# Folding the four squared-deviation subsets on GpSimd before the averaging matmul

## Chip, cores and metric

One core of a Trainium2 chip runs the whole program. The metric is the device time of one launch in microseconds.

## What is computed

The input `x` is 32 images of 512 channels, 28 x 28 pixels, float32. The reference, cut to what matters:

```python
def _gn(v, G=32, eps=1e-05):                       # group norm: 16 channels and all pixels of one image
    m = jnp.mean(g, axis=(2, 3, 4), keepdims=True)
    s = jnp.var(g, axis=(2, 3, 4), keepdims=True)
    return (g - m) / jnp.sqrt(s + eps)
...
xa = round(clip((xg - lA) / (uA - lA), 0, 1) * 15) / 15      # xg: the normed input, channel groups rotated by one
wq = (round(clip((weight - lW) / (uW - lW), 0, 1) * 15) / 15 - 0.5) * 2
y = einsum('bgihw,goi->bgohw', xa, wg)                       # 4 groups of 128 x 128, 1 x 1 convolution
y = relu(y * inv + shift)                                     # batch norm with given statistics
return x + (y + identity)                                     # identity: the normed input
```

## The kernel before, in words

Channels lie on the 128 partitions, in 4 groups (G) of 784 pixels per image. The images go through a ring of 12 buffers, `images`. Loads and the last two images' stores are issued by SyncE (L192, L200, L204, L213), the stores of images 0 to 29 by ScalarE (L263). A load beyond the twelfth waits until the store of the image that had its buffer has landed (L199).

The norm is worked out for two images at a time, a pair `u`. Per pair:

- VectorE takes partial statistics of 2 of the 4 groups (3 for the first two pairs) with `bn_stats` (L461) on half images. Each half gives two subsets, so a group has SUBSETS = 4 partial means and partial sums of squares. `sum_stats` (L469) adds them. ScalarE takes the sum and the squares of the other groups (L237, L243).
- TensorE averages across the 16 channels of a norm group with small float32 matmuls: `average_means` (L576, L577, L579). ScalarE copies the means to SBUF (L251, `gmean`).
- GpSimd takes the deviations of the subset means from the group mean (`deviations`, L376 and L379) and squares them (L383). TensorE averages the squares into `var_ps`, one matmul for each of the four subsets (`average_deviations`, L585). ScalarE forms the standard deviation (L257, L258), VectorE a rough reciprocal (L493), GpSimd refines it and forms the coefficients in seven small instructions (`coefficients`, L399 to L407).
- Per image and group, ScalarE (L271, three groups) and GpSimd (L425, one group) write int16 levels. VectorE caps them to bf16 codes, four groups at once (`cap`, L476). TensorE multiplies (`multiply`, L612, six matmuls: three parts of the weight by two halves). GpSimd turns the image into the normed one plus the input (`affine`, L414); in the last four images ScalarE does two of four (L279). VectorE adds the convolution (`finish`, L483).

`average_deviations(u)` stands in TensorE's queue between the first and the second group of an image. `keep_busy` (L593) adds six matmuls per pair whose result nobody reads. Each engine runs its own list in order, written out by hand:

- GpSimd, iteration n: coefficients (every second image), the first affine, then every second image `deviations`, the other affines, `quantise` of the next image.
- VectorE, image n: finish 0, finish 1, cap of the next image, finish 2, one half of statistics, finish 3, three halves.

A small GpSimd instruction that reads the result of the one before it waits on a semaphore for it (`linked`, L387).

Of the kernel before, what the change touches and what calls it, by code (L numbers as in the profile page):

```python
# [5 lines left out]
ALU = mybir.AluOpType  # L6
ACT = mybir.ActivationFunctionType
AXIS = mybir.AxisListType
F32 = mybir.dt.float32
# [3 lines left out]
P = 128  # L13
# [13 lines left out]
SUBSETS = 4  # L27
# [4 lines left out]
def fused_norm_quantised_conv(nc, x, weight, limits, channel_params, out):  # L32

    B, C, H, W = x.shape
    G = CONV_GROUPS
# [11 lines left out]
    def stats_on_dve(u):  # L47
        return 3 if u < 2 else 2
# [21 lines left out]
    def squares_until(u):  # L70
        return sum(2 * (G - stats_on_dve(i)) for i in range(u + 1))
# [10 lines left out]
    with ExitStack() as ctx:  # L82
        def sb(name, shape, dtype):
            return ctx.enter_context(nc.sbuf_tensor(name, shape, dtype))

        def ps(name, shape, dtype):
            return ctx.enter_context(nc.psum_tensor(name, shape, dtype))

        def sem(name):
            return ctx.enter_context(nc.semaphore(name))  # L90
# [8 lines left out]
        unused = sb("unused", [P, 2, HW], BF16)  # L99
        gmean = sb("gmean", [P, 2, 2, G], F32)  # L100
        dev = sb("dev", [P, 2, G, SUBSETS], F32)
        dev2 = sb("dev2", [P, 2, G, SUBSETS], F32)
        half_var = sb("half_var", [P, 2 * G], F32)
        std = sb("std", [P, 2, G], F32)
        rough = sb("rough", [P, 2, G], F32)
# [26 lines left out]
        avg = sb("avg", [P, P], F32)  # L132
# [5 lines left out]
        var_ps = ps("var_ps", [P, 512], F32)  # L138
# [26 lines left out]
        dev_step = sem("dev_step")  # L165
        dev_done = sem("dev_done")
        var_done = sem("var_done")
# [20 lines left out]
        @block.sync  # L188
        def _(sync):
            for n in range(SINGLE):  # L190
                for g in (0, G - 1, 1, 2):
                    sync.dma_start(images[:, n, g], x_v[n][:, g]).then_inc(first_loaded[n][g], DMA)  # L192
                if n == 0:
                    sync.dma_start(w_raw[:], weight.rearrange("(g o) i -> o g i", o=P)).then_inc(weights_in, DMA)

            def load(n):
                j = n % RING
                if n >= RING:
                    sync.wait_ge(stored[j], DMA * (n // RING))  # L199
                sync.dma_start(images[:, j], x_v[n]).then_inc(x_loaded[j], DMA)  # L200

            def store(n):
                sync.wait_ge(final, G * n + G)
                sync.dma_start(out_v[n], images[:, n % RING]).then_inc(stored[n % RING], DMA)  # L204

            for n in range(SINGLE, B):
                load(n)
            for n in range(ACT_STORES, B - 1):
                store(n)
            for g in range(G):  # L210
                o = output_group(g)
                sync.wait_ge(final, G * (B - 1) + g + 1)
                sync.dma_start(out_v[B - 1][:, o], images[:, (B - 1) % RING, o]).then_inc(stored[(B - 1) % RING], DMA)  # L213
            for j in range(RING):
                stores = len(range(j, B, RING)) + (G - 1 if j == (B - 1) % RING else 0)
                sync.wait_ge(stored[j], DMA * stores)
# [113 lines left out]
        def _(pool):  # L330
            step = [0]

            def chained(ins):
# [33 lines left out]
                                    cols[:, 1].unsqueeze(1).to_broadcast([P, 2, G]),  # L367
                                    bn[:, 4].unsqueeze(1).to_broadcast([P, 2, G]), ALU.subtract)

            def deviations(u):  # L370
                k, par = stats_on_dve(u), u % 2
                pool.wait_ge(gmean_done, u + 1)
                if u >= 1:
                    pool.wait_ge(var_done, u)
                mean = gmean[:, par].unsqueeze(3)
                nc.gpsimd.tensor_tensor(dev[:, :, 0:k], stats[:, par, :, 0:k, :, 1],  # L376
                                        mean[:, :, 0:k].to_broadcast([P, 2, k, SUBSETS]), ALU.subtract)
                own = sums[:, par, 0].unsqueeze(3)
                nc.gpsimd.tensor_tensor(dev[:, :, k:G], own[:, :, k:G].to_broadcast([P, 2, G - k, SUBSETS]),  # L379
                                        mean[:, :, k:G].to_broadcast([P, 2, G - k, SUBSETS]),  # L380
                                        ALU.subtract).then_inc(dev_step, 1)
                pool.wait_ge(dev_step, u + 1)
                nc.gpsimd.tensor_tensor(dev2[:], dev[:], dev[:], ALU.mult).then_inc(dev_done, 1)  # L383

            LINKS = 6

# [172 lines left out]
        @block.tensor  # L559
        def _(pe):  # L560
            pe.wait_ge(consts_done, 1)
            pe.wait_ge(rows_in, DMA)
            nc.tensor.transpose(cols_ps[:, 0:4 * G], rows[:], ident[0:4 * G, 0:4 * G])
            pe.wait_ge(limits_in, DMA)
            nc.tensor.matmul(cols_ps[:, 4 * G:5 * G], one_row[:], limit_row[:], start=True,
                             stop=True).then_inc(cols_turned, 1)

            def average_means(u):
                k, par = stats_on_dve(u), u % 2
                pe.wait_ge(bn_summed, u + 1)  # L570
                pe.wait_ge(squared, squares_until(u))
                if u >= 1:
                    pe.wait_ge(gmean_done, u)
                    pe.wait_ge(std_done, u)
                mean = mean_ps[:, 0:2 * G].rearrange("p (j g) -> p j g", g=G)
                nc.tensor.matmul(mean[:, :, 0:k], avg[:], sums[:, par, 0, :, 0:k], start=True, stop=True)  # L576
                nc.tensor.matmul(mean[:, :, k:G], avg_one[:], sums[:, par, 0, :, k:G], start=True,  # L577
                                 stop=True).then_inc(mean_done, 1)
                nc.tensor.matmul(var_ps[:, 0:2 * G], avg_n[:], sums[:, par, 1], start=True, stop=False)  # L579

            def average_deviations(u):
                pe.wait_ge(dev_done, u + 1)
                var = var_ps[:, 0:2 * G].rearrange("p (j g) -> p j g", g=G)
                for s in range(SUBSETS):
                    done = nc.tensor.matmul(var, avg[:], dev2[:, :, :, s], start=False, stop=(s == SUBSETS - 1))  # L585
                done.then_inc(var_done, 1)

            def keep_busy(n, u):  # L590
                pe.wait_ge(gmean_done, u)
                for _ in range(FILLERS):
                    nc.tensor.matmul(mean_ps[:, 0:HALF], w_t[:, 0, 0], codes[:, n % 2, G - 1, 0:HALF], start=True, stop=True)  # L593


            def wait_affine(n, g):
                if g < G - affine_on_act(n):
                    pe.wait_ge(y_pool, (y_pool_until(n - 1) if n else 0) + g + 1)
                else:
                    pe.wait_ge(y_act, y_act_until(n - 1) + g - (G - affine_on_act(n)) + 1)  # L600

            def multiply(n, g):
                k = G * n + g
                if g == 0:
                    pe.wait_ge(capped, n + 1)
                if k >= SETS:
                    pe.wait_ge(final, k - SETS + 1)
                for part in range(PARTS):
                    for h in range(2):
                        if (part, h) == (PARTS - 1, 1):  # L610
                            wait_affine(n, g)
                        done = nc.tensor.matmul(prod[:, k % SETS, h, 0:HALF], w_t[:, part, output_group(g)],  # L612
                                                codes[:, n % 2, g, h * HALF:(h + 1) * HALF],
                                                start=(part == 0), stop=(part == PARTS - 1))
                done.then_inc(multiplied, 1)

            pe.wait_ge(w_scaled, 1)
            for g in range(G):
                turned = nc.tensor.transpose(prep_ps[:, g], w_raw[:, g], ident[:])
            turned.then_inc(w_turned, 1)  # L620
            average_means(0)
            average_deviations(0)
            pe.wait_ge(w_ready, 1)

            for n in range(-1, B - 1):
                if n < 0:
                    average_means(1)
                    multiply(0, 0)
                    average_deviations(1)
                    multiply(0, 1)  # L630
                    multiply(0, 2)
                else:
                    multiply(n + 1, 0)
                    if n % 2 and (n + 3) // 2 < PAIRS:
                        average_deviations((n + 3) // 2)
                    multiply(n + 1, 1)
                    multiply(n + 1, 2)
                    if n % 2 == 0 and (n + 4) // 2 < PAIRS:
                        keep_busy(n + 1, (n + 4) // 2)
                        average_means((n + 4) // 2)  # L640
                multiply(n + 1, 3)
# [23 lines left out]
```

## Time and profile before

| | |
|---|---|
| median of 3 runs (lowest to highest) | 258.94 us (258.55 to 259.93) |
| the profiled execution: its own time | 260.06 us |
| the profiled execution: span from first to last instruction | 258.3 us |
| VectorE, GpSimd, ScalarE busy | 234.5, 213.8, 215.8 us (91%, 83%, 84%) |
| TensorE busy (matmuls) | 181.7 us (70%) |
| moved by DMA | 103.25 MB, mean 400 GB/s |

Busy shares are means over the whole span, the start and the end with little in them included. All times inside the trace count from the first instruction.

### The profile page before, as it was taken

Reading aid. Unit: us, or ns where it says so; the run is one execution under the profiler, and the core shown is the slowest. Engines: PE = TensorE matmul, PEld = TensorE weight load, DVE = VectorE, ACT = ScalarE, POOL = GpSimd, SP = SyncE. Lnnn points to the kernel's source line nnn. Section 1 sums busy time; section 2 is a strip of 40 time slices with the busy share of each in tenths; the row PEclk is TensorE's granted clock in tenths of the full one; section 3 lists DMA queues with packets and bytes.
Section 4 is the critical chain, followed back from the end, with each engine's and each line's share of the span. In section 5 each row is a group of like instructions: output and inputs, shape, how many; then the busy total and the mean of one; then the engine's idle time right before and its main releaser. Section 6 shows DMA issues by size and latency. Waiting matters only on the chain.

```text
span 258.3 us, 3631 instructions
## 1 busy us (share of the span) xinstructions
PE 181.7 (70%) x1083; PEld 106.4 (41%) x1083; DVE 234.5 (91%) x363; ACT 215.8 (84%) x394; POOL 213.8 (83%) x340
## 2 busy tenths in 40 slices
PE   1142978687778778686868787777868687799800
PEld 0132635354444445352535444443525353455400
DVE  2898698999999999999999999999999999999910
ACT  4338898999999999999999999999999889979300
POOL 6126869999999999999999999999999999989100
PEclk9999999999999999999999999999999999999975
DMA  6999999999999999999999999999999999999992
GB/s 224 393 412 410 408 408 408 415 418 417 416 415 417 417 413 417 416 416 416 415 418 417 414 416 417 417 414 416 416 418 413 416 417 411 401 397 403 400 399 97
DMA packets 34516, 103.25 MB, mean 400 GB/s; under 512 B 1202, under 2 KB 1730, under 8 KB 34498
## 3 DMA queue, kind: packets, MB, share of 16 engines
q1 hardware_dynamic: 18624, 54.86, 53.5%
q10 hardware_dynamic: 15874, 48.18, 46.7%
q8 instruction: 8, 0.13, 0.2%
q14 instruction: 10, 0.08, 0.1%
HBM read 51.65 MB, written 51.38 MB: 399 GB/s over the span
## 4 chain that ended last, share of the span: by engine, by line
DVE 77%; issue 7%; POOL 4%; PE 4%; DMA 2%; DVEq 0%; SPq 0%; ACT 0%; ACTq 0%; POOLq 0%
DVE images L483 41%; DVE stats L461 21%; DVE codes L476 12%; DMA images<-in_x 2%; PE prod L612 2%; PE var_ps L585 2%; DVE sums L469 1%; POOL images L414 1%; POOL levels L425 1%; DVE rough L493 1%; POOL newt L399 0%; DVEq L82 0%; DVE w_raw L519 0%; SPq L192 0%; POOL dev L379 0%
## 5 line engine op out<-in xcount | busy, mean ns | idle before, releaser
L612 PE MATMUL prod<-codes,w_t 128*128 128x392 bf16 x768 | 144.8, 334 | 43.4 <-DVE codes L476 22.6
L483 DVE SCALAR_TENSOR_TENSOR images<-prod,floor,images 128x784 f32<-128x784 f32 x128 | 126.6, 1014 | 2.8 <-PE prod L612 2.8
L414 POOL TENSOR_SCALAR images<-images,coef 128x784 f32<-128x784 f32 x120 | 119.3, 1009 | 0.0
L612 PEld LDWEIGHTS prod<-codes,w_t 128*128 128x128 bf16 x768 | 70.3, 102 | 110.9 <-DVE codes L476 34.4
L271 ACT ACTIVATE levels<-images,coef 128x784 int16<-128x784 f32 x95 | 91.5, 1028 | 0.9 <-issue 0.9
L461 DVE BATCH_NORM_STATS2 stats<-images 128x6 f32<-128x392 f32 x136 | 68.7, 548 | 5.3 <-DMA images<-in_x 5.3
L237 ACT ACTIVATE unused<-images 128x784 bf16<-128x784 f32 x60 | 50.8, 847 | 7.2 <-DMA images<-in_x 5.2
L243 ACT ACTIVATE unused<-images,sums 128x784 bf16<-128x784 f32 x60 | 56.1, 939 | 0.1
L476 DVE TENSOR_SCALAR codes<-levels 128x3136 bf16<-128x3136 int16 x32 | 40.8, 1275 | 1.2 <-POOL levels L425 1.2
L425 POOL TENSOR_SCALAR levels<-images,coef 128x784 int16<-128x784 f32 x33 | 33.1, 1005 | 0.1
L376 POOL TENSOR_TENSOR dev<-stats,gmean 128x16 f32<-128x16 f32 (+1 forms) x16 | 15.2, 948 | 9.2 <-ACT gmean L251 9.2
L585 PEld LDWEIGHTS var_ps<-dev,avg 128*128 128x128 f32 x128 | 18.1, 209 | 2.7 <-POOL dev L383 1.5
L585 PE MATMUL var_ps<-dev,avg 128*128 128x8 f32 x128 | 16.9, 259 | 1.4 <-POOL dev L383 1.4
L593 PE MATMUL mean_ps<-codes,w_t 128*128 128x392 bf16 x84 | 16.2, 329 | 0.0
L403 POOL TENSOR_TENSOR norm<-gmean,norm 128x8 f32<-128x8 f32 x16 | 14.5, 904 | 1.3
L243 ACT ACTIVATION_READ_ACCUMULATOR unused<-images,sums 128x1 f32 x60 | 11.4, 191 | 0.0
L237 ACT ACTIVATION_READ_ACCUMULATOR unused<-images 128x1 f32 x60 | 11.3, 188 | 0.0
L257 ACT ACTIVATE half_var<-var_ps,eps 128x8 f32<-128x8 f32 x16 | 4.3, 267 | 7.4 <-PE var_ps L585 7.4
L593 PEld LDWEIGHTS mean_ps<-codes,w_t 128*128 128x128 bf16 x84 | 8.2, 98 | 4.8
L576 PE MATMUL mean_ps<-sums,avg 128*128 128x4 f32 (+1 forms) x32 | 5.1, 230 | 6.8 <-DVE sums L469 6.8
L576 PEld LDWEIGHTS mean_ps<-sums,avg 128*128 128x128 f32 x32 | 6.0, 205 | 8.2 <-issue 4.9
L399 POOL TENSOR_TENSOR newt<-rough 128x8 f32<-128x8 f32 x16 | 4.0, 249 | 5.5 <-DVE rough L493 5.5
(68 smaller groups left out, 88.8 us busy)
## 6 DMA issues: line engine op xcount, KB each, us to landing
images<-in_x SPq DMA_DIRECT2D x30, 1568.0 KB, 13.3
out<-images ACTq DMA_DIRECT2D x30, 1568.0 KB, 18.9
images<-in_x SPq DMA_DIRECT2D x8, 392.0 KB, 6.6
out<-images SPq DMA_DIRECT2D x1, 1568.0 KB, 11.0
out<-images SPq DMA_DIRECT2D x4, 392.0 KB, 8.0
w_raw<-in_weight SPq DMA_DIRECT2D x1, 256.0 KB, 6.6
rows<-in_channel_params ACTq DMA_DIRECT2D x1, 8.0 KB, 2.4
limit_row<-in_limits ACTq DMA_DIRECT2D x1, 0.0 KB
```

Of the source, the lines that this page charges most:

```text
L237: nc.scalar.activation(unused[:, g % 2], images[:, n % RING, g], ACT.Identity, scale=1.0 / HW, accum_out=sums[:, u % 2, 0, j, g:g + 1]).th ...
L243: nc.scalar.activation(unused[:, g % 2], images[:, n % RING, g], ACT.Square, scale=-1.0, bias=sums[:, u % 2, 0, j, g:g + 1], accum_out=sum ...
L271: nc.scalar.activation(levels[:, n % 2, g], images[:, n % RING, g], ACT.Relu, bias=coef[:, u % 2, 1, 0, G * j + g:G * j + g + 1], scale=co ...
L376: nc.gpsimd.tensor_tensor(dev[:, :, 0:k], stats[:, par, :, 0:k, :, 1], mean[:, :, 0:k].to_broadcast([P, 2, k, SUBSETS]), ALU.subtract)
L414: nc.gpsimd.tensor_scalar(here, here, coef[:, u % 2, 0, 1, G * j + o:G * j + o + 1], coef[:, u % 2, 1, 1, G * j + o:G * j + o + 1], ALU.mu ...
L425: nc.gpsimd.tensor_scalar(levels[:, n % 2, g], images[:, n % RING, g], coef[:, u % 2, 0, 0, G * j + g:G * j + g + 1], coef[:, u % 2, 1, 0, ...
L461: nc.vector.bn_stats(two, images[:, n % RING, g, h * HALF:(h + 1) * HALF]).then_inc(bn_done, 1)
L476: nc.vector.tensor_scalar(codes[:, n % 2], levels[:, n % 2], 0.0, TOP, ALU.max, ALU.min).then_inc(capped, 1)
L483: nc.vector.scalar_tensor_tensor(out=two, in0=prod[:, k % SETS, :, 0:HALF], scalar=floor[:, o:o + 1], in1=two, op0=ALU.max, op1=ALU.add).t ...
L585: done = nc.tensor.matmul(var, avg[:], dev2[:, :, :, s], start=False, stop=(s == SUBSETS - 1))
L593: nc.tensor.matmul(mean_ps[:, 0:HALF], w_t[:, 0, 0], codes[:, n % 2, G - 1, 0:HALF], start=True, stop=True)
L612: done = nc.tensor.matmul(prod[:, k % SETS, h, 0:HALF], w_t[:, part, output_group(g)], codes[:, n % 2, g, h * HALF:(h + 1) * HALF], start= ...
```

## The change

GpSimd's `deviations` gets two more instructions: after the square, subsets 0 and 1 are added to subsets 2 and 3 (32 elements to 16 per partition), and the two halves are added (16 to 8). Each waits for the one before it. TensorE's `average_deviations` then is one float32 matmul and no longer four.

```diff
-        dev2 = sb("dev2", [P, 2, G, SUBSETS], F32)
+        dev2 = sb("dev2", [P, 2 * G, SUBSETS], F32)
+        dev2_half = sb("dev2_half", [P, 2 * G, SUBSETS // 2], F32)
+        dev2_sum = sb("dev2_sum", [P, 2 * G], F32)
...
+            FOLDS = 3
+
+            def folded(u, k, ins):
+                ins.then_inc(dev_step, 1)
+                pool.wait_ge(dev_step, FOLDS * u + k)
...
-                nc.gpsimd.tensor_tensor(dev[:, :, k:G], own[:, :, k:G].to_broadcast([P, 2, G - k, SUBSETS]),
-                                        mean[:, :, k:G].to_broadcast([P, 2, G - k, SUBSETS]),
-                                        ALU.subtract).then_inc(dev_step, 1)
-                pool.wait_ge(dev_step, u + 1)
-                nc.gpsimd.tensor_tensor(dev2[:], dev[:], dev[:], ALU.mult).then_inc(dev_done, 1)
+                folded(u, 1, nc.gpsimd.tensor_tensor(dev[:, :, k:G], own[:, :, k:G].to_broadcast([P, 2, G - k, SUBSETS]),
+                                                     mean[:, :, k:G].to_broadcast([P, 2, G - k, SUBSETS]), ALU.subtract))
+                dev_ = dev[:].rearrange("p j g s -> p (j g) s")
+                folded(u, 2, nc.gpsimd.tensor_tensor(dev2[:], dev_, dev_, ALU.mult))
+                folded(u, 3, nc.gpsimd.tensor_tensor(dev2_half[:], dev2[:, :, 0:2], dev2[:, :, 2:4], ALU.add))
+                nc.gpsimd.tensor_tensor(dev2_sum[:], dev2_half[:, :, 0], dev2_half[:, :, 1], ALU.add).then_inc(dev_done, 1)
...
-                var = var_ps[:, 0:2 * G].rearrange("p (j g) -> p j g", g=G)
-                for s in range(SUBSETS):
-                    done = nc.tensor.matmul(var, avg[:], dev2[:, :, :, s], start=False, stop=(s == SUBSETS - 1))
-                done.then_inc(var_done, 1)
+                nc.tensor.matmul(var_ps[:, 0:2 * G], avg[:], dev2_sum[:], start=False, stop=True).then_inc(var_done, 1)
```

`keep_busy` and everything else stay as they are.

## Rows read from the trace of the kernel before

**Rows 1.** The page: the chain that ended last, by engine.
```profile
DVE 77%; issue 7%; POOL 4%; PE 4%; DMA 2%; DVEq 0%; SPq 0%; ACT 0%; ACTq 0%; POOLq 0%
```

**Rows 2.** Busy time of each engine in one pair's stretch, 127.05 to 141.10 us.
```profile
core 0: us, PE busy (x) PEld busy (x) DVE busy (x) ACT busy (x) POOL busy (x), PEclk, DMA share, GB/s
127.05:141.10 14.05, 11.04 (x68) 6.36 (x68) 14.02 (x22) 13.38 (x26) 13.50 (x21) 1.00 1.03 417
```

**Rows 3.** The same view, long stretches: steady part, its end, after the last issue.
```profile
41.10:214.00 172.90, 135.94 (x841) 78.58 (x841) 172.23 (x257) 163.41 (x306) 166.24 (x247) 1.00 1.03 416
214.00:240.00 26.00, 21.97 (x133) 12.09 (x130) 25.34 (x35) 24.59 (x39) 24.56 (x36) 1.00 1.03 402
...
247.75:258.30 10.55, 0.00 (x0) 0.00 (x0) 0.00 (x0) 0.00 (x0) 0.00 (x0) 0.55 0.55 214
```

**Rows 4.** DMA rate in 40 slices of 0.38 us, from 243.2 to 258.3 us.
```profile
GB/s 399 390 399 399 407 399 407 399 399 399 399 399 399 399 399 407 391 424 407 399 407 391 357 341 316 324 249 100 75 58 25 25 25 25 25 25 17 0 0 0
```

**Rows 5.** Stores and loads: issues (start us), landings, the chain's first transfer.
```profile
out<-images ACTq DMA_DIRECT2D x30, 1568.0 KB, 18.9
...
L204 SPq DMA_DIRECT2D out<-images x1: 388/388/388, 242.6 to 242.6; - x1
...
L213 SPq DMA_DIRECT2D out<-images x4: 356/866/1252, 243.5 to 246.5; - x4
...
DMA to landing us min/median/max: 7.6/8.0/11.1
...
0.79 1.81 SPq L192 DMA_DIRECT2D images<-in_x  x4
...
1.70 5.65 DMA images<-in_x
```

**Rows 6.** Timeline of GpSimd and VectorE in one pair (start us, us, engine, line).
```profile
125.52 1.01 POOL L414 TENSOR_SCALAR images<-images,coef 128x784 f32<-128x784 f32 x1
125.80 1.60 DVE L476 TENSOR_SCALAR codes<-levels 128x3136 bf16<-128x3136 int16 x1
126.48 1.00 POOL L376 TENSOR_TENSOR dev<-stats,gmean 128x16 f32<-128x16 f32 x1
...
127.73 0.24 POOL L383 TENSOR_TENSOR dev<-dev 128x32 f32<-128x32 f32 x1
127.95 2.96 POOL L414 TENSOR_SCALAR images<-images,coef 128x784 f32<-128x784 f32 x3
...
132.98 1.07 POOL L403 TENSOR_TENSOR norm<-gmean,norm 128x8 f32<-128x8 f32 x1
133.03 0.96 DVE L476 TENSOR_SCALAR codes<-levels 128x3136 bf16<-128x3136 int16 x1
...
138.58 1.01 POOL L425 TENSOR_SCALAR levels<-images,coef 128x784 int16<-128x784 f32 x1
...
139.84 1.60 DVE L476 TENSOR_SCALAR codes<-levels 128x3136 bf16<-128x3136 int16 x1
```

**Rows 7.** Groups by line: a small linked GpSimd instruction (busy, mean ns, idle before).
```profile
L400 POOL TENSOR_TENSOR newt<-newt,half_var 128x8 f32<-128x8 f32 x16 | 3.3, 206 | 1.3
```

**Rows 8.** Timeline: TensorE at the start and in a pair, and who waits.
```profile
18.23 1.87 PE L585 MATMUL var_ps<-dev,avg 128*128 128x8 f32 x8 [1.45 <-POOL dev L383]
...
26.89 2.14 PE L612 MATMUL prod<-codes,w_t 128*128 128x392 bf16 x6 [0.54 <-DVE codes L476]
...
28.82 1.71 PE L585 MATMUL var_ps<-dev,avg 128*128 128x8 f32 x8
...
33.77 0.82 POOL L399 TENSOR_TENSOR newt<-rough 128x8 f32<-128x8 f32 x1 [2.47 <-DVE rough L493]
...
127.46 1.17 PE L612 MATMUL prod<-codes,w_t 128*128 128x392 bf16 x6 [0.87 <-DVE codes L476]
...
128.46 0.95 PE L585 MATMUL var_ps<-dev,avg 128*128 128x8 f32 x8
...
227.80 0.27 ACT L257 ACTIVATE half_var<-var_ps,eps 128x8 f32<-128x8 f32 x1 [1.31 <-PE var_ps L585]
```

## Prediction

> **What bounds the kernel now.** I read the chain that ended last first. It gives VectorE 77% and DMA 2% [rows 1]. Taken alone, that says a VectorE-bound kernel. The windows by engine say more. One pair of images takes 14.05 us, and VectorE is busy for 14.02 of it [rows 2]. I read six such stretches between 43 and 226 us; all are 14.04 or 14.05 us long. GpSimd is busy for 13.50 us. The rest, 0.55 us, is the seven gaps of about 0.08 us in its linked instructions (1.3 us over 16 pairs for each such line [rows 7]). So GpSimd never waits for anybody either. Two engines are full at once.
>
> The timeline shows why. The cap (L476) takes 0.96 us at 133.03 but 1.60 us at 125.80, where a GpSimd affine began at 125.52 and ended at 126.53. The cap was done 0.87 us after that end, at 127.40. The GpSimd instruction behind the affine, 16 elements per partition, took 1.00 us, from 126.48 to 127.48 [rows 6]. Each of the two has to wait until the other's instruction is over. VectorE loses some 0.7 us per pair in this, counted as busy, so its own work is about 13.3 us. GpSimd loses about 0.8 us twice per pair (L376 and L403), and it cannot avoid that. **GpSimd, not VectorE, sets the 14.05 us.**
>
> The third reading is DMA. It is full (share 1.03) from 41.1 to 214 us at 416 GB/s and to 240 us at 402 GB/s [rows 3]. The last store is issued by 247.75 us; after that no engine works, and transfers go on for 10 us [rows 3, 4]. So compute is ahead of DMA, and what ends the span is the backlog of stores. In the middle a store of 1568 KB lands 18.9 us after its issue [rows 5], where its own share at 400 GB/s is 4.0 us. The chain does not show this backlog, as it follows VectorE to its last instruction.
>
> **The change part by part.**
>
> *GpSimd, per pair.* Two more instructions of 16 and 8 elements. The nearest row is L400, 206 ns [rows 7]. Each also adds one gap of 0.08 us. That makes 2 x 0.29 = 0.58 us. Bounds: 0.41 us if the gaps vanish, 0.64 us if each takes the 240 ns of the square [rows 6]. Behind them in the queue are three affines and a quantise, then the coefficients. The GpSimd queue issues no DMA. Waiting for the cap absorbs nothing: shifted by 0.58 us, another small instruction meets the cap and is held as long. From 134 us on, GpSimd runs to the quantise that ends at 139.59, and the cap at 139.84 waits for the affine behind it [rows 6]. With GpSimd 0.58 us later, the cap finds its levels late (at 140.17), waits for them, and then for the affine that has already begun. So the pair becomes 14.63 us. That holds for pairs 2 to 14, in which GpSimd is full: 13 x 0.58 = +7.5 us.
>
> *TensorE.* A float32 matmul shows as two records, so eight go to two. In a pair the eight take 0.95 us [rows 8], so 0.7 us goes. It pays the 0.58 us for the variance, which comes 0.1 us earlier, not later; nobody on the full engines waits for that. Its remaining cover is VectorE's own order, since the reciprocal is taken there only at 131 us.
>
> *Start.* Before the steady part, TensorE is on the path and slow: six matmuls take 2.14 us at 26.89 us and 1.17 us at 127.46 us [rows 8]; the first is the pace of 1.2 GHz, the second that of 2.4 GHz. Of pair 0's eight (1.87 us) six go: 1.40 less 0.58 is 0.8 us earlier. Of pair 1's eight (1.71 us) six go, 1.28 us; there GpSimd's extra is free, as it idled 2.47 us before L399 [rows 8]. Together 2.1 us earlier. ScalarE's statistics of image 3 stand between, so I take 1.6 us. Bounds: 1.3 (pair 1 alone), and 2.5 if TensorE also reaches its full pace sooner.
>
> *End, pair 15.* ScalarE waited 1.31 us for the variance [rows 8]. It comes some 0.4 us earlier there, and ScalarE's list sets the pace behind it. I take -0.3 us; bounds -0.4 and +0.3.
>
> *Sum for compute:* -1.6 + 7.5 - 0.3 = **+5.6 us** at the last stores. From below 13 x 0.41 - 2.5 - 0.4 = +2.4, from above 13 x 0.64 - 1.3 + 0.3 = +7.3 us.
>
> *What DMA makes of it.* Image 30's store is issued at 242.6 us [rows 5]. From issue to the first packet I take 0.9 us (the first load, issued at 0.79, moves at 1.70 [rows 5]). Two images are then left at the least, 2 x 4.0 us. So the last landing cannot be before 251.5 us plus the shift. Now it is at 246.5 + 11.1 = 257.6 us [rows 5]. The shift has to pass **6.0 us** before the end moves. That this is so is seen in the last slices: 400 GB/s to about 251 us, then some 3 us at 25 GB/s [rows 4], a sixteenth of the rate: one DMA engine of 16 is behind, and a later issue of the others' work costs it nothing. With +5.6 us the end stays: span 258.3, own time 260.06 us.
>
> The median of the runs is 1.1 us below that profiled execution. If DMA was quicker in those by as much and compute was not, the slack there is 4.9 us, and 0.7 us comes through: 259.6 us. If the whole execution was quicker, it stays 258.94. I take the middle, **259.3 us**.
>
> One figure from the Trainium skill speaks against this. DMA: Bandwidth & Descriptors, Where 436 GB/s comes from, puts the port ceiling at 435 GB/s. At that rate 103.25 MB would take 237 us, and DMA would not cover the end. The trace does not agree, the rate being flat at 416 and 402 GB/s with every engine full; the measurement decides.
>
> **The rivals.**
>
> 1. *The delay comes through (slower).* Place: the issue of the last two stores. It decides from 6.0 us of shift in the profiled execution, from about 4.9 us in a median one. With +7.3 us, 1.3 to 2.4 us come through: 260.2 to 261.4 us, by the likelier middle 260.8. For it: the margin is only 0.4 us in my sum, and both engines are full. Against it: the start gives back over 1.3 us. Chance 0.28.
>
> 2. *DMA is not the end at all (slower by the full compute shift).* If transfers were full only because they are issued early, and caught up when compute is slower, the end would move with compute: 258.94 + 5.6 = 264.5 us. This is also what the skill's 435 GB/s would give. Against it: the rate a 14.63 us pair asks for, 4 x 1.606 MB, is 439 GB/s, above the 416 it gets, so the backlog still grows. Chance 0.04.
>
> 3. *TensorE's clock falls.* The granted clock is 1.00 in the pair, with TensorE busy 11.04 of 14.05 us [rows 2]; afterwards it is 10.3 of 14.63. If it fell to 1.2 GHz, 48 matmuls of a pair would take 0.16 us more each (2.14 against 1.17 us for six [rows 8]), 7.8 us, and the six unread ones 1.0 us: 19.1 us a pair, +66 us, 325 us. Against it: the gaps between its groups stay near 1 us. TensorE: Matmul & The Clock Gate, Part 1, says an idle stretch halves the clock; no stretch here becomes idle. Chance 0.03.
>
> 4. *GpSimd absorbs the adds.* If a held instruction is shorter for having been issued later, pairs stay 14.05 us and compute ends 1.9 us earlier; DMA is full anyway. 258.9 us. Against it: both held ones end 0.06 to 0.08 us behind the cap, with 16 elements or 8 [rows 6]. Chance 0.10.
>
> **How the numbers follow.** 0.5% is 1.3 us, about what a measurement of this kernel can tell from no change. The forecast, the backlog hides it, has 0.55; it falls within 0.5%, as does rival 4. Rival 1 lies on both sides of the bound; I give slower most of it, and to the forecast's case 0.04 for faster, a run spread like the one of before. Faster 0.06, same 0.64, slower 0.30. The range reaches from the low end of the spread, 258.2, to the upper end of rival 1, 261.5 us; rivals 2 and 3 are left out.
>
> **What would show it.** GpSimd busy +6.6 us (32 x 0.206). Pairs of 14.63 us, with VectorE now idle some 0.3 us a pair before L476 for the levels of L425, which is 1.2 us in all now. Stores 30 and 31 issued about 5.6 us later, transfers after the last issue down from 10 us to about 5. Pairs of 14.05 us would make the compute step wrong; a span that ends over 1.3 us later with stores issued less than 6 us later would make the backlog step wrong.

## The result, and the profile after

The change made the kernel slower. Its median is 261.58 us over 6 runs (261.27 to 262.01), against 259.05 us (258.55 to 259.93) for the kernel before on the same chip. The ratio is 1.0095, with a 95% interval of 1.0079 to 1.0111. The forecast of no change did not hold, and the median lies just above the range given. It is the side of rival 1. Here and below an execution over 1.5% above the shortest of its kernel is left out of a ratio, which concerns only three executions of one kernel of run 9.

The profiled execution has a time of 261.27 us and a span of 259.5 us, 1.8 us less, as before the change (260.06 and 258.3). It is the shortest of its six, while that of before was the longest of its kernel's, so the two profiles differ by 1.2 us only. The page's chain that ended last:

```profile
POOL 67%; issue 8%; PE 6%; DMA 6%; DVE 5%; SPq 2%; ACT 2%; DVEq 0%; POOLq 0%
```

In [rows 1] VectorE had 77%. Now GpSimd (POOL) has the chain. The same pair as in [rows 2], by engine:

```profile
127.05:141.68 14.63, 10.62 (x64) 5.57 (x63) 14.25 (x22) 13.41 (x26) 13.93 (x23) 1.00 1.03 416
```

GpSimd's two new instructions and their gaps fill the pair as before; VectorE now has 0.38 us to spare. The timeline of the pair answers to [rows 6]:

```profile
126.73 1.00 POOL L423 TENSOR_SCALAR images<-images,coef 128x784 f32<-128x784 f32 x1
126.86 1.75 DVE L485 TENSOR_SCALAR codes<-levels 128x3136 bf16<-128x3136 int16 x1 [0.34 <-POOL levels L434]
127.69 0.99 POOL L384 TENSOR_TENSOR dev<-stats,gmean 128x16 f32<-128x16 f32 x1
...
129.25 0.22 POOL L391 TENSOR_TENSOR dev_half<-dev 128x16 f32<-128x16 f32 x1
129.55 0.20 POOL L392 TENSOR_TENSOR dev_sum<-dev_half 128x8 f32<-128x8 f32 x1
...
134.20 1.06 POOL L410 TENSOR_TENSOR newt<-three_halves,newt 128x8 f32<-128x8 f32 x1
134.23 0.96 DVE L485 TENSOR_SCALAR codes<-levels 128x3136 bf16<-128x3136 int16 x1
```

Two things forecast from [rows 6] stand here. The cap (L485) waits for the levels, 0.34 us, and then for the affine that began before it. And the instruction that the second cap holds is now L410 and no longer L403, held for as long.

The start and the end of the steady part are read from GpSimd's first deviation of pairs 2 and 15. Before the change (L376):

```profile
42.19 0.99 POOL L376 TENSOR_TENSOR dev<-stats,gmean 128x16 f32<-128x16 f32 x1
...
224.81 1.01 POOL L376 TENSOR_TENSOR dev<-stats,gmean 128x16 f32<-128x16 f32 x1
```

After it (L384), with the matmuls of pairs 0 and 1, and the last stores and their landings:

```profile
18.49 0.60 PE L592 MATMUL var_ps<-dev_sum,avg 128*128 128x8 f32 x2 [2.02 <-POOL dev_sum L392]
...
27.80 0.43 PE L592 MATMUL var_ps<-dev_sum,avg 128*128 128x8 f32 x2
...
39.91 0.99 POOL L384 TENSOR_TENSOR dev<-stats,gmean 128x16 f32<-128x16 f32 x1
...
230.08 0.99 POOL L384 TENSOR_TENSOR dev<-stats,gmean 128x16 f32<-128x16 f32 x1
...
248.02 0.39 SPq L206 DMA_DIRECT2D out<-images  x1
...
L215 SPq DMA_DIRECT2D out<-images x4: 356/870/1257, 249.0 to 251.9; - x4
...
DMA to landing us min/median/max: 6.3/6.4/6.9
```

Pair 2 is 2.3 us earlier, 13 pairs take 190.2 us and no longer 182.6, so pair 15 begins 5.3 us later. Image 30's store is issued 5.4 us later (248.0 against 242.6 in [rows 5]). The last landing moved from 257.6 to 258.8 us. Where DMA was full to the end [rows 3, 4], it now is not:

```profile
214.00:224.00 10.00, 7.24 (x42) 3.56 (x42) 9.65 (x14) 9.55 (x21) 9.29 (x18) 1.00 1.03 405
224.00:250.00 26.00, 21.77 (x130) 11.89 (x129) 25.18 (x31) 19.46 (x24) 20.57 (x29) 1.00 0.88 344
```

From 224 to 250 us the rate falls to 344 GB/s: stores come too late, and DMA waits for compute. The backlog is used up.

### The profile page after: what moved, and what is told of

Its sections match the earlier page's. It is cut to its first block, busy times and chain, and to the rows that moved or that the text cites. A ratio compares the mean times of both kernels' runs of the same rounds, so it can differ in the third digit from the quotient of the medians.

```text
span 259.5 us, 3471 instructions
## 1 busy us (share of the span) xinstructions
PE 177.9 (69%) x987; PEld 95.2 (37%) x987; DVE 237.5 (92%) x363; ACT 215.3 (83%) x394; POOL 218.4 (84%) x372
## 4 chain that ended last, share of the span: by engine, by line
POOL 67%; issue 8%; PE 6%; DMA 6%; DVE 5%; SPq 2%; ACT 2%; DVEq 0%; POOLq 0%
POOL images L423 35%; POOL levels L434 10%; DMA images<-in_x 6%; POOL newt L410 6%; PE prod L618 5%; POOL dev L384 5%; DVE images L492 4%; SPq L194 2%; POOL norm L412 1%; POOL coef L416 1%; POOL scaled L414 1%; POOL dev L390 1%; DVE codes L485 1%; POOL newt L408 1%; POOL newt L409 1%
## 5 line engine op out<-in xcount | busy, mean ns | idle before, releaser
L618 PE MATMUL prod<-codes,w_t 128*128 128x392 bf16 x768 | 150.1, 343 | 52.3 <-DVE codes L485 19.5
L618 PEld LDWEIGHTS prod<-codes,w_t 128*128 128x128 bf16 x768 | 71.4, 104 | 122.9 <-DVE codes L485 30.8
L485 DVE TENSOR_SCALAR codes<-levels 128x3136 bf16<-128x3136 int16 x32 | 42.3, 1322 | 6.1 <-POOL levels L434 5.4
L384 POOL TENSOR_TENSOR dev<-stats,gmean 128x16 f32<-128x16 f32 (+1 forms) x16 | 13.1, 818 | 11.0 <-ACT gmean L253 11.0
L253 ACT ACTIVATE gmean<-mean_ps 128x8 f32<-128x8 f32 x16 | 2.8, 173 | 16.9 <-PE mean_ps L586 16.9
L410 POOL TENSOR_TENSOR newt<-three_halves,newt 128x8 f32<-128x8 f32 x16 | 14.3, 897 | 1.3
L245 ACT ACTIVATION_READ_ACCUMULATOR unused<-images,sums 128x1 f32 x60 | 11.4, 191 | 0.0
L592 PEld LDWEIGHTS var_ps<-dev_sum,avg 128*128 128x128 f32 x32 | 5.5, 205 | 6.8 <-POOL dev_sum L392 6.5
L281 ACT ACTIVATE images<-images,coef 128x784 f32<-128x784 f32 x8 | 7.6, 1030 | 0.0
L592 PE MATMUL var_ps<-dev_sum,avg 128*128 128x8 f32 x32 | 6.3, 268 | 2.0 <-POOL dev_sum L392 2.0
```

The lines of the kernel that those rows point to most:

```text
L245: nc.scalar.activation(unused[:, g % 2], images[:, n % RING, g], ACT.Square, scale=-1.0, bias=sums[:, u % 2, 0, j, g:g + 1], accum_out=sum ...
L410: linked(u, 3, nc.gpsimd.tensor_tensor(newt[:, 2], three_halves[:], newt[:, 1], ALU.subtract))
L485: nc.vector.tensor_scalar(codes[:, n % 2], levels[:, n % 2], 0.0, TOP, ALU.max, ALU.min).then_inc(capped, 1)
```

## The experiments

A time below is the median of a kernel's executions, a ratio is to the kernel before on the same chip, with its 95% interval. Lengths of pairs, spans and positions are those of the one profiled execution. "Store 30" is the issue of image 30's store there, "tail" the time from there to the end of the span. In runs 1 to 5 and 7 these lines, given in outline, take the place of the fixed counts:

```diff
+    def adds(u):      # adds on GpSimd for pair u: 0, 1 (four subsets to two), 2 (to one)
+    def matmuls(u):   # averaging matmuls for pair u: 4, 2 or 1
...
-                nc.tensor.matmul(var_ps[:, 0:2 * G], avg[:], dev2_sum[:], start=False, stop=True).then_inc(var_done, 1)
+                for s in range(matmuls(u)):
+                    done = nc.tensor.matmul(var, avg[:], squares(s), start=False, stop=(s == matmuls(u) - 1))
+                done.then_inc(var_done, 1)
```

**1. TensorE's half alone**: adds 0, matmuls 1. The squares of three of the four subsets are left out of the variance.

> TensorE's half of the change alone: one averaging matmul, of the first subset's squares (the other three subsets' squares are left out of the variance), and no adds on GpSimd. Theory A (GpSimd sets the pair, the DMA backlog hides compute until the last stores are issued too late; then the end is the issue of image 30's store plus 11.5 us): pairs stay 14.05 us, the start is about 2.9 us earlier, image 30's store is issued at about 239.5 us, and nothing of it is seen in the time: 259.0 us, within 0.6. Rival B (compute sets the end, DMA only looks full): 3 us faster, 256 us. Rival C (the lower granted clock of the changed kernel costs the time): slower than before, 260 us or more, since TensorE has as little work as in the changed kernel.

Measured: 258.46 us, ratio 0.9969 (0.9955 to 0.9982), store 30 at 241.73 us, span 256.8. Pair 2 was at 39.26 us, 2.9 us earlier than before, and pairs took 14.05 us up to pair 12. Then they took 14.5 to 15.4 us. In the line of pair 14 GpSimd is no longer full:

```profile
209.55 0.22 POOL L391 TENSOR_TENSOR dev<-stats,gmean 128x16 f32<-128x16 f32 x1 [1.68 <-ACT gmean L259]
```

ScalarE was late there because it had waited for loads (4.4 us between 190 and 240 us). Compute had caught up with DMA's supply. Store 30 was 0.9 us earlier and not 3. Of the 2.9 us at the start, 0.7 came through in the time; why it is not nothing, as in run 5, is not shown. Rivals B and C fall: compute does not set the end of the kernel before, and TensorE's lighter load (clock 0.962 to 0.976) does not make it slower.

**2. GpSimd's half alone**: adds 2, matmuls 4, which read `dev2`.

> GpSimd's half alone: both adds run, but TensorE still averages all four subsets with four matmuls, so the variance is the reference's and the adds' result is read by nobody. Theory A: pairs 14.63 us, no gain at the start, image 30's store at about 251.0 us (8.4 later than before), end 11.5 us behind it, 264.3 us. Rival B: 259 + 8.4 = 267.5 us. Rival C (clock): TensorE has all its work and the clock stays at 1.00, so 259 us.

Measured: 263.03 us, ratio 1.0152 (1.0138 to 1.0165). Pairs of 14.62 us, store 30 at 250.90 us, as worked out; the tail is 10.1 us and not 11.5, so the time is 1.3 us under the expected one. The slowdown is there at a mean clock of 0.982 in the profile, that of the kernel before.

**3. Half the change**: adds 1, matmuls 2.

> Half the change: one add on GpSimd (four subsets to two), two averaging matmuls. Theory A: pairs 14.34 us (+0.29), start about 1.5 us earlier, image 30's store at about 244.9 us (+2.3), under the point where the end moves: 259.0 us. Rival B: 259 + 2.3 = 261.3 us. A version for use if A holds and it is not slower.

Measured: 259.05 us, ratio 0.9994 (0.9980 to 1.0007), pairs 14.34 us, store 30 at 244.49 us. Compute 1.9 us later costs nothing.

**4. The change in pairs 0 to 11**: `adds(u)` is 2 if u < 12, else 0.

> The change in pairs 0 to 11, the old four matmuls in pairs 12 to 15. Ten steady pairs pay 0.58 us: image 30's store at about 242.6 - 2.3 + 5.8 = 246.1 us. Theory A: 246.1 + 11.5 = 257.6 us span, 259.4 us time, just at the knee. Rival B: 259 + 3.5 = 262.5 us.

Measured: 258.86 us, ratio 0.9985 (0.9974 to 0.9997), store 30 at 247.36 us and not at 246.1. The profiled execution is the longest of this kernel's (span 257.9; the median one is 257.1). In it the granted clock was 0.50 from 92 to 99 us, and the two pairs around it took 30.0 us and not 29.25. With a tail of 10.5 us in the median one too, an estimate, some 4 to 4.8 us of shift are still hidden.

**5. The change in pairs 0 and 1 alone**: `adds(u)` is 2 if u < 2, else 0.

> The change in pairs 0 and 1 alone, where TensorE is on the path and GpSimd has room; the old four matmuls in the other 14 pairs. Theory A: the start is 2.3 us earlier (GpSimd's first deviation of pair 2 at about 39.9 us, 42.19 before), pairs 14.05 us until compute meets the loads, as in the run with the matmuls alone; DMA sets the end: 258.5 us, 0.2 to 0.3% under before. If it is so, it beats both kernels. Rival B (compute sets the end): 259.1 - 2.3 = 256.8 us.

Measured: 258.55 us, ratio 0.9993 (0.9976 to 1.0011). Pairs of 14.03 us from 40.31 us on, then 16.0 us for the last. No gain: DMA sets the end. This is the best version that computes everything, and it does not differ from the kernel before.

**6. Half of each store left out** (two of the four channel groups, images 0 to 30), in the kernel before and in the changed one. The output is incomplete; all computation runs.

```diff
-                sync.dma_start(out_v[n], images[:, n % RING]).then_inc(stored[n % RING], DMA)
+                sync.dma_start(out_v[n][:, 0:2], images[:, n % RING, 0:2]).then_inc(stored[n % RING], DMA)
...
-                    act.dma_start(out_v[n], images[:, n % RING]).then_inc(stored[n % RING], DMA)
+                    act.dma_start(out_v[n][:, 0:2], images[:, n % RING, 0:2]).then_inc(stored[n % RING], DMA)
```

> The kernel before, but of images 0 to 30 only channel groups 0 and 1 are stored (the other two groups' output is left out), so DMA has 25 MB less to move and no backlog. All computation runs. Theory A: compute as before, image 30's store at about 242.6 us, the end now some 7 us behind it: about 251.5 us.

> The changed kernel with the same half of the stores left out. Theory A: image 30's store at 248.0 us and the end 7 us behind it, 257 us: without the DMA backlog the change costs its whole compute shift, 5.4 us against the half-store version of before, and not 2.5. Rival D (the 2.5 us is all that the change costs, and the later stores are an artefact of waiting for DMA): 2.5 us between the two.

Measured: 251.25 us (250.91 to 251.99) and 256.98 us (256.71 to 257.86). The change now costs 5.7 us in the medians and 5.0 us in the two profiles (spans 250.2 and 255.2), where store 30 is 5.0 us later: the whole compute shift. Store 30, first of the kernel before, then of the changed one:

```profile
242.13 0.39 SPq L204 DMA_DIRECT2D out<-images  x1
```

```profile
247.11 0.39 SPq L206 DMA_DIRECT2D out<-images  x1
```

Both spans end 8.1 us behind it. DMA moved 291 and 288 GB/s from 60 to 240 us there. Rival D falls. The 2.5 us of the full kernel are what is not hidden of 5.0 to 5.7 us.

**7. Twice the adds**: `adds(u)` is 4, matmuls 1.

> The changed kernel with the two adds made twice (four small linked instructions more than before the change, the second two write the same values). Theory A: pairs 15.2 us, image 30's store at 248.0 + 7.5 + 0.3 = 255.8 us, span 10.3 us behind it, time about 268 us: now that the backlog is used up, every microsecond comes through. A theory in which the backlog still hides part would give less than 266 us.

Measured: 267.75 us, ratio 1.0322 (1.0297 to 1.0347), store 30 at 255.09 us, span 266.5. Against the changed kernel store 30 is 7.1 us later and the median 6.2 us. Past the backlog, nearly all of a delay comes through. The tail is 11.4 us here, as the last store is issued 5.4 us behind store 30 (260.5 less 255.1) and not 3.9 as in the changed kernel. Pairs are 15.02 us and not 15.2; the second two adds cost 0.39 us.

**8. No square**: the kernel before without L383; the matmuls average `dev`.

```diff
-                                        ALU.subtract).then_inc(dev_step, 1)
-                pool.wait_ge(dev_step, u + 1)
-                nc.gpsimd.tensor_tensor(dev2[:], dev[:], dev[:], ALU.mult).then_inc(dev_done, 1)
+                                        ALU.subtract).then_inc(dev_done, 1)
```

> The kernel before without the square on GpSimd: the matmuls average the deviations themselves, so the variance leaves out the squares. It takes one linked instruction of 0.24 us and one gap from GpSimd. Theory A (GpSimd sets the pair): pairs 13.75 us until compute meets the loads, then the DMA's own pace; time 258.5 us. A theory in which VectorE sets the pair: pairs stay 14.05 us.

Measured: 258.88 us, ratio 0.9996 (0.9977 to 1.0015), and pairs of 13.48 us. GpSimd does set the pair. But an instruction and its gap, some 0.32 us, taken out gave 0.57. These lines of the run show where the rest is:

```profile
103.20 0.99 DVE L474 TENSOR_SCALAR codes<-levels 128x3136 bf16<-128x3136 int16 x1
103.43 0.86 POOL L405 TENSOR_TENSOR coef<-scaled,coef_add 128x32 f32<-128x32 f32 x1
...
110.04 1.00 DVE L474 TENSOR_SCALAR codes<-levels 128x3136 bf16<-128x3136 int16 x1
```

GpSimd's instruction arrives 0.23 us after the cap's begin, and so is held 0.61 us (0.86 less its own 0.25), not the 0.87 of L403 in [rows 6]. The other cap, begun just before the affine's end, takes 1.00 us and not 1.60. What the two engines lose to each other depends on the moment at which they meet. The page SBUF — State Buffer of the Trainium skill (section SBUF: two separate sides) has it as an exclusive lock, held for the whole instruction by whichever started first; the durations agree, and add that it is the phase that sets the price.

**9. TensorE's clock.** The changed kernel's granted clock is 0.947 to 0.976 in its six executions, that of before 0.977 to 0.989 in 87. In the profile it falls from 2.4 to 1.2 GHz (1.00 to 0.50) four times for 3.4 us in the steady part, where the kernel before has no fall. Two runs were to give TensorE its work back: 12 unread matmuls per pair, and three unread small ones behind the one that is left.

```diff
-FILLERS = 6
+FILLERS = 12
```

> The changed kernel with 12 unread matmuls per pair and not 6, which gives TensorE back more work than the change took. Theory A: granted clock back at about 0.98, pairs 14.63 us as before them, image 30's store at 248.0 us, 261.6 us. Rival C (the lower clock costs time): with the clock back, the time falls towards 259 us.

Measured: 260.25 us, ratio 1.0046 (1.0021 to 1.0071), times from 258.57 to 262.65 us, clock 0.945 to 0.978. This tells nothing on rival C, as the longer burst did not bring the clock back. Its profile, which is its longest execution, has pairs of 13.7 to 16.9 us, some of them waiting for the means that the unread matmuls stand in front of. That the median is under the changed kernel's is not explained; the undisturbed pairs are 14.54 to 14.55 us in that profile and not 14.62.

```diff
                 nc.tensor.matmul(var_ps[:, 0:2 * G], avg[:], dev2_sum[:], start=False, stop=True).then_inc(var_done, 1)
+                for _ in range(SUBSETS - 1):
+                    nc.tensor.matmul(mean_ps[:, 0:2 * G], avg[:], avg_n[:, 0:2 * G], start=True, stop=True)
```

> The changed kernel with three small float32 matmuls, which nobody reads, behind the one that is left, so TensorE does as many as before the change, at the same place. Theory A: the granted clock is back near 0.98, pairs 14.63 us, image 30's store at about 248 to 249 us (the start loses part of its gain, as the unread ones are again on TensorE's path there), time 261.5 to 262.5 us: the lower clock of the changed kernel costs nothing. Rival C (the dips of the clock cost the time): back towards 259.5 us.

Measured: 261.07 us, ratio 1.0077 (1.0060 to 1.0095), pairs of 14.62 us, store 30 at 249.05 us, span 259.2. The clock is 0.979 in the profile, with two falls left of four, and 0.968 to 0.981 in all. Most of the clock is back and the time is not. Rival C falls, by the changed kernel's own trace above all. Two of its four falls change no pair. Behind the other two the means come late, and GpSimd waits 0.80 us for them, but then its deviation takes 0.23 us and not 0.99, as the cap is over. That makes one pair 15.46 us and the next 13.83, together 29.29, where two normal ones are 29.25: 0.04 us for such a fall. Only a longer fall has a price, as in run 4 (0.75 us).

**10. The tail.** The changed kernel's tail is 11.5 us; in runs 2, 4 and 9 it is 10.1 to 10.5. The DMA view of the changed kernel, 249.0 to 259.5 us in 40 slices, shows one engine of 16 that ends last (24 GB/s is a sixteenth):

```profile
GB/s 406 394 406 394 442 394 406 394 394 406 394 418 430 418 394 382 394 418 406 394 406 430 418 382 382 394 418 418 442 347 24 24 24 24 24 12 0 0 0 0
```

And from 244 to 246 us, where the store of image 29 begins, the view by queue has the first of these lines, and from 249.0 us on the second (q10 is ScalarE's queue, with the stores of images 0 to 29):

```profile
q8 instruction: 1, 0.02, 5.2%
...
q10 hardware_dynamic: 11, 0.03, 0.8%
```

5.2% of 16 engines for 2 us are 1.66 us of one engine: an instruction fetch of 16 KB, begun at 244.3 us beside the first packets. At 249.0 us, when the last stores have begun, 11 packets of image 29's are still to come. At 24 GB/s those 0.03 MB are some 1.4 us of one engine, by which one ends last.

```diff
+            for _ in range(100):
+                pe.wait_ge(consts_done, 1)
```

> The changed kernel with 100 extra waits on a semaphore that has long been set, in TensorE's list near its start, where it idles 7 us. They compute nothing. Open is why the changed kernel ends 11.5 us behind image 30's store and the others 10.1 to 10.5. Theory E: one 16 KB instruction fetch on one DMA engine, at 244.3 us in the changed kernel, takes 1.7 us there just as the store of image 29 begins, after DMA had run dry, so that engine is last by 1.5 us. If the fetched code is TensorE's, 100 more instructions bring the fetch about 10 us earlier, where the engine still finds a gap to catch up; the span then ends 10.1 to 10.5 us behind image 30's store, at 258.3 us, time 260.1 to 260.6 us. Rival F (the tail is that long for another reason, or the code is another engine's): 261.6 us.

Measured: 259.92 us (258.69 to 261.19), ratio 1.0018 (1.0001 to 1.0035). Store 30 is at 247.90 us, where it was, and the span ends 10.5 us behind it. In the same view, 249 to 259 us, 2 packets of image 29's store are left, and hardly an engine is behind at the end:

```profile
GB/s 427 401 401 401 401 401 401 389 414 414 389 414 414 401 414 377 427 414 401 402 401 389 414 402 401 414 414 414 401 426 339 38 13 0 0 0 0 0 0 0
```

This kernel does the whole change, its stores come as late, and yet most of the slowdown is gone. By the two profiles 1 us of the slowdown hangs on the tail, by the two ratios nearly 2 of 2.5, and not on GpSimd. The mechanism is only half shown. The fetch moved, but from 244.3 to 243.3 us and not by 10 us (the 100 waits became 49 instructions of 51 ns), which puts nearly all of it in front of the store's first packets instead of beside them; it then takes 0.93 us. That the engine with the fetch is the one that ends last is not shown. That the code fetched is TensorE's is inferred from the spacing of the fetches: some 26 us before the change and 29 us after it, as TensorE's list per pair shrinks by the code from 136 to 124 matmuls and weight loads. Runs 1 and 2 bear it out: with GpSimd's list as before and TensorE's shorter it is 28.2 us, with GpSimd's longer and TensorE's as before 26.9 us. How often the fetch meets the store, and what it costs in the median, stays open: this kernel's times spread over 2.5 us, those of the changed one over 0.7 us.

## Why the prediction was wrong, point by point

- **What bounds the pair: right.** GpSimd sets it. Run 8 shortened it, run 2 lengthened it with TensorE's work unchanged, and the chain went over to GpSimd.
- **The price of the adds: right.** 216 and 203 ns with gaps of 0.08 us gave pairs of 14.63 us. GpSimd's busy time rose by 4.6 us and not by 6.6, as its first deviation was no longer held in pair 1 and in the two pairs behind a fall of the clock (L384 has 13.1 us in all, L376 had 15.2). That waiting for the cap absorbs nothing held here, but not in general (run 8, run 7).
- **Start and end: small errors that cancel, which is luck.** The start gave 2.3 us (I took 1.6), pair 15 gave +0.15 us (I took -0.3). The sum is +5.4 us at image 30's store; +5.6 was forecast. That TensorE runs at 1.2 GHz at 26.89 us I took from durations; the granted clock that the profile shows for 26 to 30 us is 1.00, so no row bears it out.
- **What DMA makes of it: the step that failed.** "The shift has to pass 6.0 us" came from a tail of 0.9 + 8.0 = 8.9 us from image 30's store to the last landing (by its own figures 6.1: 257.6 less 251.5). Measured, that tail is 10.8 us (248.02 to 251.9 + 6.9) in the changed kernel, and 9.5 to 9.9 us in runs 2, 4, 10 and the second of 9, where compute sets the end as well. I summed bytes over a rate and gave nothing to the way from the last packet to the landing (about 0.4 us, by the slices of run 10), nor to the time in which one DMA engine ends behind the others. So 0.6 to 1.0 us were missing in general, and 0.9 to 1.3 more in this kernel, which is the part that run 10 removes and only half explains. The profiled execution had 4.2 us of slack (257.6 less 242.6 and 10.8), not 6.0.
- **The basis: taken by halves.** The profile of before is at the slow end of its kernel's executions: 87 spans of it go from 256.2 to 258.3 us, and their median is 257.3. If DMA alone makes that spread, which is argued and not shown (only one execution has a profile), a median execution has 1.0 us less slack, 3.2 us, and 5.4 - 3.2 = 2.2 us come through; 2.5 were measured. The same sum with each kernel's own tail gives 3.8 us for run 2 (3.9 measured), 2.0 for the unread small matmuls of run 9 (2.0) and 1.2 for run 10 (0.7). I had written this case down, but took the middle between it and no delay at all. With the usual tail of 9.5 to 9.9 us it gives 0.9 to 1.3 us, a time of 260.0 to 260.4 us, inside the range. By this sum it is the longer tail of this one kernel that put the result outside.
- **The rivals.** Rival 1 came true with its mechanism and place, 0.2 us above its upper figure of 261.4. Rival 2 is refuted by runs 1, 3 and 6, rival 3 by run 9 (the clock does fall, but for short stretches that cost 0.04 us at most), rival 4 by the pairs of 14.63 us.

## What to carry to other kernels

When transfers run on for long after the last engine has stopped, as here, the chain of waits names the wrong resource. Work out how late the last issues may come, and take the tail behind them from a trace in which compute does set the end (or leave out part of the transfers, as in run 6, to see compute alone). Allow for its spread: here it was 10.1 to 11.5 us to the end of the span, and a hundred idle waits in TensorE's list took 1.0 us off it. Take the slack from a median execution. And an engine that is busy all the time need not set the pace: VectorE was busy for 14.02 of 14.05 us because GpSimd held it.

## What was not expected of the hardware

- TensorE's granted clock fell four times for 3.4 us after six of its eight small variance instructions per pair were gone, though it was busy for 10.6 of 14.6 us. The number of those instructions is not all: run 2, which has all eight and longer pairs, shows two falls. Behind two of the four falls GpSimd waited 0.80 us and got nearly all of it back.
- The DMA engines do not end together: in the kernel before one of them is some 3 us behind [rows 4], in the changed one 1.5 us, in run 2 none. Instruction fetches of 16 KB each take 0.9 to 1.9 us of one engine. In the changed kernel such a fetch fell on the start of a store.
- An instruction of 0.24 us and its gap less on GpSimd gave 0.57 us per pair, and two more adds with gaps, of 0.58 us, gave 0.39, since the meetings with VectorE's cap moved.
